# A macaron block (feed-forward, attention, feed-forward): the projections as sums of 16-bit products, and the rope sum one block later

## The chip, the cores and the metric

One Trainium2 chip, one of its cores. The metric is the device time of one execution in microseconds (us), as the median of several. In what follows PE is TensorE (PEld its weight loads), DVE is VectorE, ACT is ScalarE, POOL is GpSimd and SP is the engine that issues the DMAs.

## The reference

4 batches of 1024 rows of width 512 go through three residual layers. The first and the last are a feed-forward layer with ternary weights. The middle one is attention with 32 query heads and 8 key and value heads of 16 columns:

```
x = x + 0.5 * ffn(layernorm(x), w_gate_up, w_proj)
x = x + attn(layernorm(x), Wq, bq, Wk, bk, Wv, bv, Wo, bo)
x = x + 0.5 * ffn(layernorm(x), w_gate_up, w_proj)

Q, K, V = x @ Wq.T + bq, x @ Wk.T + bk, x @ Wv.T + bv
Q, K = Q * cos + rot_half(Q) * sin, K * cos + rot_half(K) * sin
out = softmax(Q @ K.T / 4) @ V @ Wo.T + bo
```

All of it is in 32-bit floats. The change concerns the line that makes Q, K and V.

## The kernel before, in words

The kernel runs five stages, one behind the other: `first_layer`, `projections`, `attention`, `attention_output` and `ffn`. Between them every engine waits for all the others.

**Projections** work on 32 blocks of 128 rows (`NSUB`). The 512 columns of a row meet a weight of 512 x 768 (`w_qkv`: `FQ` = 512 columns for the queries, then 128 for the keys, together `FA` = 640, then 128 for the values, in all `FALL` = 768). For one block these happen, with the line in brackets:

1. DVE takes the statistics of the rows (`row_stats`, L1312, and `row_moments`, L1316 and L1318), POOL the inverse root (`root`, L1363), DVE scales the rows (`normalise`, L1323).
2. PE turns the rows, four squares of 128 (`turn`, L1402), into PSUM (`turn_ps`), and ACT copies them to `xt` (`copy_turned`, L1384).
3. PE multiplies `xt` by `w_qkv` (`product`, L1411): for 512 and for 256 columns four matmuls each, on 32-bit operands. Each of these stands in the trace as two.
4. DVE adds the bias, 768 columns from PSUM (`add_bias`, L1331). SP stores the 128 columns of the values (L1287).
5. The rope: DVE multiplies 640 columns by the cosines (`cosine`, L1336), while POOL makes the sine terms in two operations of 320 columns (`sine`, L1372). DVE adds the two (`rotate`, L1343).
6. PE turns the 640 sums, five squares (`features`, L1420), ACT keeps a 16-bit part of them (`high_part`, L1391), DVE the 16-bit rest (`low_part`, L1348), and SP stores both for every second block (L1304). In the last eight steps SP also issues the first loads of the attention stage.

The order is written out by hand by `steps`: in step j each engine handles, for each stage of its list, the block j minus the stage's lag, in the order of the list. The first 8 steps and those behind the last block are written out, the 24 between are a loop of 8. DVE's list is

```
steps(nc, dve, NSUB, [(0, row_stats), (0, stats_made), (5, low_part), (0, row_moments),
                  (1, normalise), (3, add_bias), (3, cosine), (3, rotate)], unroll=RX, peel=RX)
```

PE has turn at 2, product at 3 and features at 4; ACT copy_turned at 2 and high_part at 5; POOL root at 0 and sine at 3. Semaphores count the blocks: `biased` is raised by add_bias and waited for by cosine and sine, `cosines` and `sines` by rotate, `roped` by features, `lows` (of the block before) by features.

**Balance.** In `first_layer`, while its second tile of 512 rows is worked on, the class `Balance` finds a power of two for the query weights and its inverse for the key weights: DVE takes largest magnitudes (`measure_queries`, `measure_rest`, L111 to L117), PE adds them over the partitions (`total_over_rows`, L122), DVE makes exponents and factors in a chain of operations on one or two columns (`take_factors`, L126 to L142) and later scales the weights (`apply`, L147). These stand between DVE's `hidden` operations (L413), one for each of the 16 parts of a tile.

Of the kernel before, what the change touches and what calls it, by code (L numbers as in the profile page):

```python
# [82 lines left out]
class Balance:  # L83
# [3 lines left out]
    def __init__(self, nc, ctx, w_qkv, bias, w_in, ones):  # L87
# [6 lines left out]
        self.parts = [(w_qkv[:, :, 0:FQ], bias[:, 0:FQ]), (w_qkv[:, :, FQ:FA], bias[:, FQ:FA])]  # L94
        self.w_in, self.ones = w_in, ones
        self.largest = sb("largest", [P, 4], F32)
        self.total = sb("total", [P, 4], F32)
        self.size = sb("size", [P, 2], F32)
        self.exponent = sb("exponent", [P, 2], mybir.dt.int32)
# [13 lines left out]
    def measure_rest(self, dve):  # L113
        w, b = self.parts[1]
        dve.tensor_reduce(self.largest[:, 1:2], w, AX.XY, ALU.max, apply_absolute_value=True).then_inc(self.measured, 1)
        for k in range(2):
            dve.tensor_reduce(self.largest[:, 2 + k:3 + k], self.parts[k][1], AX.X, ALU.max,  # L117
                              apply_absolute_value=True).then_inc(self.measured, 1)

    def total_over_rows(self, pe, ps):  # L120
        pe.wait_ge(self.measured, 4)
        pe.matmul(ps[:, 0:4], self.ones, self.largest[:], start=True, stop=True).then_inc(self.summed, 1)  # L122

    def take_factors(self, dve, ps):
        dve.wait_ge(self.summed, 1)
        dve.tensor_copy(self.total[:], ps[:, 0:4]).then_inc(self.copied, 1)  # L126
        dve.wait_ge(self.copied, 1)
        dve.tensor_tensor(self.size[:], self.total[:, 0:2], self.total[:, 2:4], ALU.add).then_inc(self.sizing, 1)
# [98 lines left out]
def first_layer(nc, units, squares, square, neg_half, wt, rows, src, dst, stored, ident, ones, hidden_range, balance,  # L227
# [12 lines left out]
    with ExitStack() as ctx:  # L240
# [130 lines left out]
        def _(dve):  # L371
# [90 lines left out]
            def tile(t, k, next_rows=True, c0=0):  # L462
                second = isinstance(t, int) and t == 1
                for c in range(c0, HC):
# [754 lines left out]
def projections(nc, x, rope, x_in, load, w_qkv, bias, w_in, qk_parts, v_rows, ident, neg_half,  # L1219
# [7 lines left out]
    with ExitStack() as ctx:  # L1227
# [81 lines left out]
        def _(dve):  # L1309
# [45 lines left out]
            steps(nc, dve, NSUB, [(0, row_stats), (0, stats_made), (5, low_part), (0, row_moments),  # L1355
                              (1, normalise), (3, add_bias), (3, cosine), (3, rotate)], unroll=RX, peel=RX)
# [608 lines left out]
def macaron(nc, x, units, w_qkv_t, b_qkv, w_o_t, b_o, rope, squares, out):  # L1965
# [8 lines left out]
    with ExitStack() as ctx:  # L1974
# [36 lines left out]
        with ExitStack() as outer:  # L2011
            output_in = OutputInput(nc, outer, ctx, rows, x1, att, den, inv)
            with ExitStack() as inner:
# [57 lines left out]
```

## Time and profile before

| | |
|---|---|
| median of 3 runs | 3099.67 us (3096.92 to 3100.73) |
| the profiled execution's own time | 3102.39 us |
| its span, first to last instruction | 3100.6 us, mean granted TensorE clock 0.982 of full |
| busy: PE, PEld, DVE, ACT, POOL | 2960.6, 1213.7, 1890.7, 1731.7, 749.6 us |
| `first_layer` | to about 779 us |
| `projections` | 779.7 to 1003 us |
| `attention` | to about 2265 us |
| `attention_output`, then `ffn` | to about 2385 us, then to the end |

The profile is of one execution, which took 2.72 us more than the median. Times in its rows are from the span's start. A row of the timeline reads: start, length of the run of like instructions, engine, line, operation, output and inputs, count, and in brackets how long the engine was idle before and what ended that. PE's lengths include the way through the array, so that successive ones overlap; the distance between starts is what one costs.

### The profile page before, as it was taken

Reading aid. Unit: us, or ns where it says so; the run is one execution under the profiler, and the core shown is the slowest. Engines: PE = TensorE matmul, PEld = TensorE weight load, DVE = VectorE, ACT = ScalarE, POOL = GpSimd, SP = SyncE. Lnnn points to the kernel's source line nnn. Section 1 sums busy time; section 2 is a strip of 40 time slices with the busy share of each in tenths; the row PEclk is TensorE's granted clock in tenths of the full one; section 3 lists DMA queues with packets and bytes.
Section 4 is the critical chain, followed back from the end, with each engine's and each line's share of the span. In section 5 each row is a group of like instructions: output and inputs, shape, how many; then the busy total and the mean of one; then the engine's idle time right before and its main releaser. Section 6 shows DMA issues by size and latency. Waiting matters only on the chain. (4 is left out here: it accounts for less than half of the span.)

```text
span 3100.6 us, 61131 instructions
## 1 busy us (share of the span) xinstructions
PE 2960.6 (95%) x20310; PEld 1213.7 (39%) x20310; DVE 1890.7 (61%) x2349; ACT 1731.7 (56%) x3156; POOL 749.6 (24%) x644
## 2 busy tenths in 40 slices
PE   7889999999998999999999999999997999999999
PEld 4444444444564122222222222222233444444444
DVE  7853222221676999999999999999723222222221
ACT  5733333333111599999999999999910333333332
POOL 0154444444443000000000000000022444444444
PEclk9999999999999799999999999999998999999999
DMA  4311110011333011111111111111256011111100
GB/s 132 116 43 41 41 41 14 26 41 42 92 106 102 11 34 31 30 30 30 31 31 30 30 30 30 30 31 31 95 181 227 5 42 41 41 41 41 41 14 28
DMA packets 163902, 160.56 MB, mean 52 GB/s; under 512 B 62552, under 2 KB 100824, under 8 KB 163808
## 3 DMA queue, kind: packets, MB, share of 16 engines
q1 hardware_dynamic: 163808, 159.30, 17.4%
q8 instruction: 60, 0.98, 0.1%
q14 instruction: 34, 0.28, 0.0%
HBM read 111.48 MB, written 47.19 MB: 51 GB/s over the span
## 5 line engine op out<-in xcount | busy, mean ns | idle before, releaser
L1756 DVE TENSOR_REDUCE at_neg_max<-at_max_ps 128x1 f32<-128x1024 f32 x1024 | 1172.6, 1206 | 19.8 <-PE at_max_ps L1634 19.0
L1742 ACT ACTIVATE at_probs<-at_score_ps 128x512 f32<-128x512 f32 x2048 | 1112.9, 597 | 81.9 <-PE at_score_ps L1654 37.8
L1663 PE MATMUL at_out_ps<-at_probs,at_v 128*32 128x256 f32 x8192 | 655.0, 391 | 24.4 <-ACT at_out L1728 24.0
L1634 PE MATMUL at_max_ps<-at_km,at_q 48*128 48x512 f16 x2048 | 633.0, 390 | 13.9 <-PEq L1227 8.2
L1654 PE MATMUL at_score_ps<-at_q,at_ks 50*128 50x512 f16 x2048 | 622.0, 382 | 15.0 <-DMA at_q<-at_max_parts 9.3
L983 DVE SCALAR_TENSOR_TENSOR f_h<-f_up_ps,hr_factor,f_gate 128x512 f32<-128x512 f32 x128 | 96.1, 751 | 478.1 <-ACT f_gate L1057 475.9
L1945 POOL TENSOR_TENSOR rows<-rows,bias 128x512 f32<-128x512 f32 x32 | 39.5, 1265 | 1353.2 <-ACTq L1880 1272.8
L1654 PEld LDWEIGHTS at_score_ps<-at_q,at_ks 50*128 50x128 f16 x2048 | 164.4, 93 | 434.8 <-ACT at_probs L1742 394.7
L413 DVE SCALAR_TENSOR_TENSOR f_h<-f_up_ps,hr_factor,f_gate 128x512 f32<-128x512 f32 x112 | 83.9, 749 | 393.9 <-PE f_up_ps L752 240.8
L1663 PEld LDWEIGHTS at_out_ps<-at_probs,at_v 128*32 128x32 f32 x8192 | 161.6, 108 | 402.1 <-issue 219.7
L1057 ACT ACTIVATE f_gate<-f_gate_ps 128x512 f32<-128x512 f32 x128 | 76.4, 597 | 354.3 <-PE f_up_ps L1130 354.3
L1079 POOL TENSOR_TENSOR f_h_lo<-f_h,f_h_hi 128x512 f16<-128x512 f32 x128 | 148.2, 1158 | 379.3 <-ACT f_h_hi L1046 379.3
L752 PE MATMUL f_gate_ps<-f_xt_hi,wt 128*128 128x512 f16 x512 | 195.7, 382 | 13.1 <-ACT f_gate L588 12.5
L770 PE MATMUL f_out_ps<-wt,f_h_hi 128*128 128x512 bf16 x512 | 195.0, 381 | 9.6 <-DVE rows L430 5.3
L661 POOL TENSOR_TENSOR f_h_lo<-f_h,f_h_hi 128x512 f16<-128x512 f32 x112 | 130.8, 1168 | 302.1 <-ACT f_h_hi L605 302.0
L1130 PE MATMUL f_gate_ps<-f_xt_hi,wt 128*128 128x512 f16 x512 | 195.1, 381 | 8.3 <-ACT f_gate L1057 6.9
L1144 PE MATMUL f_out_ps<-wt,f_h_hi 128*128 128x512 bf16 x512 | 194.1, 379 | 1.6 <-POOL f_h_lo L1079 1.6
L752 PE MATMUL f_gate_ps<-f_xt_lo,wt 128*128 128x512 f16 x512 | 195.3, 381 | 0.0
L770 PE MATMUL f_out_ps<-wt,f_h_lo 128*128 128x512 bf16 x512 | 195.1, 381 | 0.0
L1130 PE MATMUL f_gate_ps<-f_xt_lo,wt 128*128 128x512 f16 x512 | 195.1, 381 | 0.0
L1130 PE MATMUL f_up_ps<-f_xt_hi,wt 128*128 128x512 f16 x512 | 194.3, 379 | 0.0
L1130 PE MATMUL f_up_ps<-f_xt_lo,wt 128*128 128x512 f16 x512 | 194.1, 379 | 0.0
(148 smaller groups left out, 3722.5 us busy)
## 6 DMA issues: line engine op xcount, KB each, us to landing
rows<-x SPq DMA_DIRECT2D x40, 1024.0 KB, 5.6
x<-rows SPq DMA_DIRECT2D x16, 1024.0 KB, 4.6
f_raw<-units SPq DMA_DIRECT2D x48, 256.0 KB, 2.6
at_q<-qk_parts SPq DMA_DIRECT2D x384, 32.0 KB, 1.7
rows<-x SPq DMA_DIRECT2D x32, 256.0 KB, 2.8
at_q<-at_max_parts SPq DMA_DIRECT2D x512, 1.0 KB
att<-at_out SPq DMA_DIRECT2D x256, 32.0 KB
out<-rows SPq DMA_DIRECT2D x8, 1024.0 KB, 4.2
```

Source lines behind the costliest of these rows:

```text
L661: nc.gpsimd.tensor_tensor(h_lo[:, c % HR, :], h[:, c % HB, :], h_hi[:, c % HR, :], ALU.subtract).then_inc(hlos, 1)
L752: last = nc.tensor.matmul(ps[:], wt[:, 2 * c + n, d, :], part[:, k, d, :], start=(d == 0 and part is xt_hi), stop=(d == DC - 1 and part is ...
L770: last = nc.tensor.matmul(out_ps[s][:], part[:, c % HR, s * P:(s + 1) * P], wt[:, 2 * HC + (c // DC) * DC:2 * HC + (c // DC) * DC + DC, c ...
L983: nc.vector.scalar_tensor_tensor(out=h[:, c % HB, :], in0=up_ps[:], scalar=hidden_range.factor, in1=gate[:, c % 2, :], op0=ALU.mult, op1=A ...
L1079: nc.gpsimd.tensor_tensor(h_lo[:, c % HR, :], h[:, c % HB, :], h_hi[:, c % HR, :], ALU.subtract).then_inc(hlos, 1)
L1130: last = nc.tensor.matmul(ps[:], wt[:, 2 * c + n, d, :], part[:, k, d, :], start=(d == 0 and part is xt_hi), stop=(d == DC - 1 and part is ...
L1144: last = nc.tensor.matmul(out_ps[s][:], part[:, c % HR, s * P:(s + 1) * P], wt[:, 2 * HC + (c // DC) * DC:2 * HC + (c // DC) * DC + DC, c ...
L1634: done = nc.tensor.matmul(max_ps[u % 2][:, half * QB:(half + 1) * QB], q[k][rows, j // SLOTS, h * QB + c * P:h * QB + (c + 1) * P], km[k][ ...
L1654: nc.tensor.matmul(score_ps[pos % RING][:], ks[k][rows, kc * P:(kc + 1) * P], q[k][rows, j // SLOTS, h * QB:(h + 1) * QB], start=True, sto ...
L1663: last = nc.tensor.matmul(out_ps[2 * HD * j:2 * HD * (j + 1), cols], v[k][:, kc, :], probs[:, kc % PBUF, j, cols], start=(kc == 0 and part ...
L1742: nc.scalar.activation(probs[:, kc % PBUF, j, :], score_ps[pos % RING][:], ACT.Exp, scale=HD ** -0.5).then_inc(exps, 1)
L1756: nc.vector.tensor_reduce(neg_max[:, h, column:column + 1], max_ps[u % 2][:], AX.X, ALU.max, negate=True).then_inc(maxed, 1)
```

## The change

The operands of the product become 16-bit floats, each number as a high part and the rest. Of the four products of parts the one of the two rests is left out, so each matmul becomes three.

- The weights are split once, when the stage begins: ACT writes `w_hi` (two activations, 4 x 640 and 4 x 128 columns), DVE `w_lo` (`low_weights`, two operations), in its list behind `low_turned` of block 0. The weights are first multiplied by powers of two, one for queries and keys and one for the values, so that they fill the range of 16 bits. PE waits for both before its first product.
- Of each block ACT's copy now makes `xt_hi`, and a new DVE operation, `low_turned`, makes `xt_lo` from PSUM and `xt_hi`.
- `product` has 24 matmuls on 16-bit operands instead of 8 on 32-bit ones.
- `add_bias` also takes the power of two out again: two operations (640 and 128 columns) with a factor for each partition, instead of one of 768.
- DVE's list begins with low_turned at lag 2 and rotate at lag 4, where rotate stood last at lag 3.
- Balance measures the value weights and bias too (two more maxima) and makes the powers of two in a chain of seven small operations (`take_ranges`, in part 9 of the second tile).

```diff
+    def take_ranges(self, dve):
+        dve.tensor_tensor(self.top[:, 0:1], self.exponent[:, 1:2], self.exponent[:, 0:1],
+                          ALU.subtract).then_inc(self.sizing, 1)
+        dve.tensor_scalar(self.top[:, 1:2], self.exponent[:, 2:3], 0.0, None, ALU.add).then_inc(self.sizing, 1)
+        dve.wait_ge(self.sizing, 9)
+        dve.tensor_scalar(self.held[:], self.top[:], 20.0, 250.0, ALU.max, ALU.min).then_inc(self.sizing, 1)
...
+        dve.tensor_scalar(self.lowering_bits[:], self.lower_by[:], 23, None, ALU.logical_shift_left).then_inc(self.sizing, 1)
...
+                        if c == 9:
+                            balance.take_ranges(dve)
...
-                nc.vector.tensor_tensor(rows[:, k, :], row_ps[k][:, 0:FALL], bias, ALU.add).then_inc(biased, 1)
+                for n, (c0, c1) in enumerate(((0, FA), (FA, FALL))):
+                    last = nc.vector.scalar_tensor_tensor(
+                        out=rows[:, k, c0:c1], in0=row_ps[k][:, c0:c1], scalar=balance.lowering[:, n:n + 1],
+                        in1=bias[:, c0:c1], op0=ALU.mult, op1=ALU.add)
+                last.then_inc(biased, 1)
+
+            def low_weights(n, c0, c1):
+                dve.wait_ge(w_high, n + 1)
+                nc.vector.scalar_tensor_tensor(
+                    out=w_lo[:, :, c0:c1], in0=w_qkv[:, :, c0:c1], scalar=balance.raising[:, n:n + 1],
+                    in1=w_hi[:, :, c0:c1], op0=ALU.mult, op1=ALU.subtract).then_inc(w_low, 1)
+
+            def low_turned(i, k):
+                k %= 2
+                dve.wait_ge(turned_high, i + 1)
+                nc.vector.tensor_tensor(xt_lo[:, k], turn_ps[k][:], xt_hi[:, k], ALU.subtract).then_inc(copied, 1)
+                if isinstance(i, int) and i == 0:
+                    low_weights(0, 0, FA)
+                    low_weights(1, FA, FALL)
...
-            steps(nc, dve, NSUB, [(0, row_stats), (0, stats_made), (5, low_part), (0, row_moments),
-                              (1, normalise), (3, add_bias), (3, cosine), (3, rotate)], unroll=RX, peel=RX)
+            steps(nc, dve, NSUB, [(2, low_turned), (4, rotate), (0, row_stats), (0, stats_made), (5, low_part), (0, row_moments),
+                              (1, normalise), (3, add_bias), (3, cosine)], unroll=RX, peel=RX)
...
-                nc.scalar.copy(xt[:, k % 2], turn_ps[k % 2][:]).then_inc(copied, 1)
+                nc.scalar.copy(xt_hi[:, k % 2], turn_ps[k % 2][:]).then_inc(turned_high, 1)
...
+            for n, (c0, c1) in enumerate(((0, FA), (FA, FALL))):
+                nc.scalar.activation(w_hi[:, :, c0:c1], w_qkv[:, :, c0:c1], ACT.Copy,
+                                     scale=balance.raising[:, n:n + 1]).then_inc(w_high, 1)
...
+                if isinstance(i, int) and i == 0:
+                    pe.wait_ge(w_low, 2)
                 for c0, c1 in ((0, FQ), (FQ, FALL)):
                     for c in range(DC):
-                        last = nc.tensor.matmul(row_ps[k][:, c0:c1], xt[:, k, c, :], w_qkv[:, c, c0:c1],
-                                                start=(c == 0), stop=(c == DC - 1))
+                        for x_part, w_part in ((xt_hi, w_hi), (xt_hi, w_lo), (xt_lo, w_hi)):
+                            last = nc.tensor.matmul(row_ps[k][:, c0:c1], x_part[:, k, c, :], w_part[:, c, c0:c1],
```

How DVE's instructions stand in a step of the loop, before (from the bias sum of one block to the scaling of rows before the next bias sum; names are those of the code, and what a row waits for is in its brackets):

```order
L1331 TENSOR_TENSOR pj_rows<-pj_row_ps,bias 128x768 [waits pj_prods,pj_v_out0]
L1336 TENSOR_TENSOR pj_cosd<-pj_rows,pj_rope 128x640 [waits pj_biased]
L1343 TENSOR_TENSOR pj_cosd<-pj_cosd,pj_sind 128x640 [waits pj_sines,pj_cosines]
L1312 BN_STATS pj_stats<-rows 128x6 [waits pj_x_in4]
L1352 REGISTER_ALU
L1348 TENSOR_TENSOR pj_low<-pj_feat_ps,pj_high 128x5x128 [waits pj_highs,pj_stat]
L1316 BN_AGGR pj_mv<-pj_stats 128x2
L1318 TENSOR_SCALAR pj_var_eps<-pj_mv 128x1 [waits pj_aggr]
L1323 TENSOR_SCALAR rows<-rows,pj_mv,pj_rstd 128x512 [waits pj_rstds]
```

And the same stretch of DVE in the changed kernel:

```order
L1365 SCALAR_TENSOR_TENSOR pj_rows<-pj_row_ps,bl_lowering,bias 128x640 [waits pj_prods,pj_v_out1,pj_feats]
L1365 SCALAR_TENSOR_TENSOR pj_rows<-pj_row_ps,bl_lowering,bias 128x128
L1387 TENSOR_TENSOR pj_cosd<-pj_rows,pj_rope 128x640 [waits pj_biased]
L1379 TENSOR_TENSOR pj_xt_lo<-pj_turn_ps,pj_xt_hi 128x512 [waits pj_turned_high]
L1394 TENSOR_TENSOR pj_cosd<-pj_cosd,pj_sind 128x640 [waits pj_sines,pj_cosines]
L1345 BN_STATS pj_stats<-rows 128x6 [waits pj_x_in5]
L1403 REGISTER_ALU
L1399 TENSOR_TENSOR pj_low<-pj_feat_ps,pj_high 128x5x128 [waits pj_highs,pj_stat]
L1349 BN_AGGR pj_mv<-pj_stats 128x2
L1351 TENSOR_SCALAR pj_var_eps<-pj_mv 128x1 [waits pj_aggr]
L1356 TENSOR_SCALAR rows<-rows,pj_mv,pj_rstd 128x512 [waits pj_rstds]
```

The bias sum became two operations, and between the cosine product and the rope sum (L1343, now L1394) one operation more stands, low_turned (L1379). Otherwise the rope sum has the neighbours that it had.

DVE at the start of the stage in the changed kernel, from the scaling of block 0's rows to that of block 1's:

```order
L1356 TENSOR_SCALAR rows<-rows,pj_mv,pj_rstd 128x512 [waits pj_rstds]
L1379 TENSOR_TENSOR pj_xt_lo<-pj_turn_ps,pj_xt_hi 128x512 [waits pj_turned_high]
L1372 SCALAR_TENSOR_TENSOR pj_w_lo<-w_qkv,bl_raising,pj_w_hi 128x4x640 [waits pj_w_high]
L1372 SCALAR_TENSOR_TENSOR pj_w_lo<-w_qkv,bl_raising,pj_w_hi 128x4x128 [waits pj_w_high]
L1345 BN_STATS pj_stats<-rows 128x6 [waits pj_x_in2]
L1349 BN_AGGR pj_mv<-pj_stats 128x2 [waits pj_stat]
L1351 TENSOR_SCALAR pj_var_eps<-pj_mv 128x1 [waits pj_aggr]
L1356 TENSOR_SCALAR rows<-rows,pj_mv,pj_rstd 128x512 [waits pj_rstds]
```

Before, the second, third and fourth of these rows weren't there. PE turns block 1 before its first product, and waits for this last scaling.

## Rows read from the trace of the kernel before

**Rows 1.** Waits in the projection stage: who waits for whom, us, times, longest

```profile
DVE pj_cosd L1343 <- POOL pj_sind L1372: 52.7, 32, 1.9
...
DVE pj_rows L1331 <- PE pj_row_ps L1411: 9.9, 4, 7.4
```

**Rows 2.** Timeline of DVE and of POOL, one step of the loop

```profile
849.73 0.95 DVE L1331 TENSOR_TENSOR pj_rows<-pj_row_ps,bias 128x768 f32<-128x768 f32 x1
850.71 0.83 DVE L1336 TENSOR_TENSOR pj_cosd<-pj_rows,pj_rope 128x640 f32<-128x640 f32 x1
853.17 0.82 DVE L1343 TENSOR_TENSOR pj_cosd<-pj_cosd,pj_sind 128x640 f32<-128x640 f32 x1 [1.63 <-POOL pj_sind L1372]
...
856.10 0.95 DVE L1331 TENSOR_TENSOR pj_rows<-pj_row_ps,bias 128x768 f32<-128x768 f32 x1
...
850.76 2.31 POOL L1372 TENSOR_TENSOR pj_sind<-pj_rows,pj_rope 128x320 f32<-128x320 f32 x2 [0.55 <-DVE pj_rows L1331]
```

**Rows 3.** Timeline of PE: a step of the loop, then the first two full steps

```profile
849.23 0.74 PE L1420 MATMUL pj_feat_ps<-square,pj_cosd 128*128 128x128 f32 x5
849.87 0.66 PE L1402 MATMUL pj_turn_ps<-square,rows 128*128 128x128 f32 x4
850.36 5.33 PE L1411 MATMUL pj_row_ps<-w_qkv,pj_xt 128*128 128x512 f32 x16
...
792.89 5.33 PE L1411 MATMUL pj_row_ps<-w_qkv,pj_xt 128*128 128x512 f32 x16
...
799.04 5.33 PE L1411 MATMUL pj_row_ps<-w_qkv,pj_xt 128*128 128x512 f32 x16
```

**Rows 4.** Chain that ended last: eight 16-bit matmuls of 512 columns

```profile
2429.39 1.73 PE f_out_ps L1144 x8
```

**Rows 5.** Groups of DVE's instructions by form; behind the bar busy us, mean ns

```profile
L983 DVE SCALAR_TENSOR_TENSOR f_h<-f_up_ps,hr_factor,f_gate 128x512 f32<-128x512 f32 x128 | 96.1, 751 | 478.1 <-ACT f_gate L1057 475.9 <-issue 2.1
L974 DVE TENSOR_TENSOR f_xt_lo<-f_turn_ps,f_xt_hi 128x512 f16<-128x512 f32 x32 | 21.8, 682 | 3.1 <-ACT f_xt_hi L1040 3.1
L1764 DVE SCALAR_TENSOR_TENSOR at_max_parts<-at_score_ps,at_max_parts 16x128 f16<-16x128 f32 x64 | 17.8, 278 | 2.2
```

**Rows 6.** Timeline of DVE and POOL in the last layer, at the same time

```profile
2583.99 2.73 DVE L1000 SCALAR_TENSOR_TENSOR rows<-f_out_ps,f_inv,rows 128x512 f32<-128x512 f32 x4 [0.29 <-PE f_out_ps L1144]
...
2584.51 1.16 POOL L1079 TENSOR_TENSOR f_h_lo<-f_h,f_h_hi 128x512 f16<-128x512 f32 x1 [4.34 <-ACT f_h_hi L1046]
```

**Rows 7.** Timeline, start of the stage: DVE, ACT, PE

```profile
782.20 0.69 DVE L1312 BATCH_NORM_STATS2 pj_stats<-rows 128x6 f32<-128x512 f32 x1
...
783.09 0.58 ACT L1384 COPY pj_xt<-pj_turn_ps 128x512 f32<-128x512 f32 x1 [13.74 <-PE pj_turn_ps L1402]
783.80 1.11 PE L1402 MATMUL pj_turn_ps<-square,rows 128*128 128x128 f32 x4 [0.74 <-DVE rows L1323]
...
784.71 7.91 PE L1411 MATMUL pj_row_ps<-w_qkv,pj_xt 128*128 128x512 f32 x16
```

**Rows 8.** Timeline of DVE: first and last bias sum of the 32

```profile
792.66 0.96 DVE L1331 TENSOR_TENSOR pj_rows<-pj_row_ps,bias 128x768 f32<-128x768 f32 x1 [7.45 <-PE pj_row_ps L1411]
...
989.45 0.96 DVE L1331 TENSOR_TENSOR pj_rows<-pj_row_ps,bias 128x768 f32<-128x768 f32 x1 [0.70 <-PE pj_row_ps L1411]
```

**Rows 9.** Timeline of the DMA queue at the stage's end

```profile
990.43 0.37 SPq L1287 DMA_DIRECT2D v_rows<-pj_rows  x1
...
1002.71 0.53 SPq L1304 DMA_DIRECT2D qk_parts<-pj_low  x1
```

**Rows 10.** Timeline of DVE in part 10 of the second tile, first layer

```profile
228.92 0.75 DVE L413 SCALAR_TENSOR_TENSOR f_h<-f_up_ps,hr_factor,f_gate 128x512 f32<-128x512 f32 x1 [3.52 <-issue]
```

**Rows 11.** Windows: length, PE, PEld, DVE, ACT, POOL busy; granted clock, DMA share, GB/s

```profile
10.00:20.00 10.00, 7.57 (x39) 4.91 (x39) 8.59 (x23) 6.04 (x12) 1.31 (x1) 1.00 0.34 99
20.00:30.00 10.00, 6.46 (x39) 4.24 (x40) 7.44 (x18) 5.19 (x10) 0.00 (x0) 0.83 0.33 94
...
788.00:790.00 2.00, 2.00 (x4) 0.84 (x3) 0.00 (x0) 0.00 (x0) 0.00 (x0) 0.52 0.00 0
```

More of the change, by code:

```diff
@@ L92, in sem @@
             return ctx.enter_context(nc.semaphore(f"bl_{n}"))
-        self.parts = [(w_qkv[:, :, 0:FQ], bias[:, 0:FQ]), (w_qkv[:, :, FQ:FA], bias[:, FQ:FA])]
+        self.parts = [(w_qkv[:, :, c0:c1], bias[:, c0:c1]) for c0, c1 in ((0, FQ), (FQ, FA), (FA, FALL))]
         self.w_in, self.ones = w_in, ones
[L96 to L99, printed above, removed]
+        self.largest = sb("largest", [P, 6], F32)
+        self.total = sb("total", [P, 6], F32)
+        self.size = sb("size", [P, 3], F32)
+        self.exponent = sb("exponent", [P, 3], mybir.dt.int32)
+        self.top = sb("top", [P, 2], mybir.dt.int32)
+        self.held = sb("held", [P, 2], mybir.dt.int32)
+        self.raise_by = sb("raise_by", [P, 2], mybir.dt.int32)
+        self.lower_by = sb("lower_by", [P, 2], mybir.dt.int32)
+        self.raising_bits = sb("raising", [P, 2], mybir.dt.int32)
+        self.lowering_bits = sb("lowering", [P, 2], mybir.dt.int32)
+        self.raising, self.lowering = self.raising_bits[:].bitcast(F32), self.lowering_bits[:].bitcast(F32)
         self.half = sb("half", [P, 1], mybir.dt.int32)
@@ L113, in measure_rest @@
     def measure_rest(self, dve):
[L114 to L117, printed above, removed]
+        for k in (1, 2):
+            dve.tensor_reduce(self.largest[:, k:k + 1], self.parts[k][0], AX.XY, ALU.max,
+                              apply_absolute_value=True).then_inc(self.measured, 1)
+        for k in range(3):
+            dve.tensor_reduce(self.largest[:, 3 + k:4 + k], self.parts[k][1], AX.X, ALU.max,
                               apply_absolute_value=True).then_inc(self.measured, 1)
     def total_over_rows(self, pe, ps):
-        pe.wait_ge(self.measured, 4)
-        pe.matmul(ps[:, 0:4], self.ones, self.largest[:], start=True, stop=True).then_inc(self.summed, 1)
+        pe.wait_ge(self.measured, 6)
+        pe.matmul(ps[:, 0:6], self.ones, self.largest[:], start=True, stop=True).then_inc(self.summed, 1)
     def take_factors(self, dve, ps):
         dve.wait_ge(self.summed, 1)
-        dve.tensor_copy(self.total[:], ps[:, 0:4]).then_inc(self.copied, 1)
+        dve.tensor_copy(self.total[:], ps[:, 0:6]).then_inc(self.copied, 1)
         dve.wait_ge(self.copied, 1)
-        dve.tensor_tensor(self.size[:], self.total[:, 0:2], self.total[:, 2:4], ALU.add).then_inc(self.sizing, 1)
+        dve.tensor_tensor(self.size[:], self.total[:, 0:3], self.total[:, 3:6], ALU.add).then_inc(self.sizing, 1)
         dve.wait_ge(self.sizing, 1)
@@ L1216, in projection_loads, with projections @@
     return rope, x_in, load
-def projections(nc, x, rope, x_in, load, w_qkv, bias, w_in, qk_parts, v_rows, ident, neg_half,
+def projections(nc, x, rope, x_in, load, w_qkv, balance, bias, w_in, qk_parts, v_rows, ident, neg_half,
                 before, n_starts, start_next, v_out, parts_out):
@@ L1246, in projections @@
         low = sb("low", [P, 2, NF, 2 * P], F16)
+        w_hi = sb("w_hi", [P, DC, FALL], F16)
+        w_lo = sb("w_lo", [P, DC, FALL], F16)
         turn_ps = [bank(f"turn_ps{k}", [P, DC, P]) for k in range(2)]
@@ L2017, in macaron @@
                 attention_in = AttentionInput(nc, inner, qk_parts, v_rows)
-                projections(nc, rows, pj_rope, pj_in, pj_load, w_qkv, bias[:, 0:FALL], w_in, qk_parts, v_rows,
+                projections(nc, rows, pj_rope, pj_in, pj_load, w_qkv, balance, bias[:, 0:FALL], w_in, qk_parts, v_rows,
                             ident, neg_half, [(f_stored[0], NTILE * 16)], attention_in.STARTS, attention_in.start,
```

14 lines of the change are left out of this document (13 added, 1 removed).

## The prediction
> **What bounds the kernel now.** The stages don't overlap, and outside `projections` the change adds only a few small operations in `first_layer`; so the question is what sets the pace of a block in the projections. PE looks like the bound there: its product alone takes 5.33 us of a step of 6.37 [rows 3]. I checked that against the waits, then against one step of the timeline.
>
> The waits say otherwise: DVE's rope sum waits for POOL's sine terms in every one of the 32 blocks, 52.7 us in all, while DVE's bias sum waits for PE only four times [rows 1]. The timeline shows a closed ring [rows 2]. The bias sum starts at 849.73 and the cosine product at 850.71 (0.98 later). POOL starts then too, takes 2.31, and the rope sum starts at 853.17 (2.46 behind the cosine product, 1.63 of it idle). Then DVE goes through rope sum, statistics, low_part, moments and normalise without a gap, and the next bias sum starts at 856.10 (2.93). 0.98 + 2.46 + 2.93 = 6.37 us a block, with no wait for PE in it. PE needs less: in the first full steps products follow each other at 6.15 (792.89 to 799.04), and in the loop its step reads 0.64 for the features, 0.49 for the turn and the rest for the product [rows 3]. PE is close behind, but the ring DVE, POOL, DVE is the bound.
>
> **The product.** Eight matmuls on 32 bits go, 24 on 16 bits come. In the last layer eight of 512 columns take 1.73 us, 0.216 each [rows 4]. The stage has none of 256; I take half, 0.108 (bounds 0.108 and 0.216). Product: 12 x 0.216 + 12 x 0.108 = 3.89, at most 5.18. PE's step becomes 0.64 + 0.49 + 3.89 = 5.02 (at most 6.31), where it had 6.15. The 1.13 us gained lie beside the ring: worth nothing in the loop, since PE wasn't waited for. Only where DVE did wait for PE is there a gain: the three short waits of the bias sum, 9.9 - 7.4 = 2.5 us [rows 1], in the last steps, where DVE has no statistics left to take. **-2.5 us.** (With the upper bound this gain goes and nothing else changes.)
>
> **The rope sum one block later.** The list gives it lag 4 instead of 3, but it also moves from the end of a step to the beginning of the next. The order of DVE's instructions shows what that comes to: bias sum, cosine product, low_turned, rope sum. It still comes before the next block's bias sum, which is what the next sine terms wait for. So the ring stays closed, and low_turned is all that slips into the 1.63 us of waiting.
>
> **low_turned.** Like the 682 ns one of the last layer [rows 5], 0.59 from start to start. Reached 0.74 behind the cosine product's start, it ends by 1.42, against 2.46 at which the rope sum may start: 1 us of cover is left. It needs ACT's copy of the turned rows: PE's turn starts 0.14 behind the bias sum and takes 0.66 [rows 2, 3], the copy 0.58 [rows 7], so it is done near 1.4, and DVE comes to low_turned at 1.17 + 0.74 = 1.9. **0 us**; without that cover, 0.59 x 30.
>
> **The bias sum in two.** An operation of this kind, with a factor for each partition and a PSUM source, takes 751 ns for 512 columns [rows 5]; the plain one takes 0.95 for 768 [rows 2] and 0.682 for 512, so a column is 1.05 ns, and the fixed part is 0.15 plain and 0.22 here. Then 640 columns take 0.88 and 128 take 0.35. Four such in a row take 2.73 [rows 6], so the next starts 0.09 before the end. Until the cosine product: 0.88 - 0.09 + 0.35 + 0.03 = 1.17, where it was 0.98. That is +0.19 in each of 31 intervals, **+5.9 us**. Bounds: the 128-column row of 278 ns gives 0.12 (+3.7); no overlap of the two, and 0.05 more, gives 0.35 (+10.9). I take the middle, since the 751 ns row is the same operation with the same kind of factor. This term stands in the ring, in front of both the cosine product and POOL, so nothing hides it.
>
> The Trainium skill, "VectorE: DVE Perf Modes", section on the TRN2 errata, gives a PSUM-source operation 120 cycles plus one a column, whatever the operation; by that the pair would cost only about 0.04 us more than the single one, +1 us in all, and the sum below would be near +3. The rows of this kernel show the fixed part to differ by 0.07 between the two kinds, and I go by them.
>
> **The start.** ACT splits the weights in the idle time before its first copy (13.74 us idle before 783.09 [rows 7], though the stage begins only at 779.7): two activations, an estimated 3.2 us by the size of its other ones. That just fits. DVE's share doesn't. Behind low_turned of block 0 (783.75 to 784.35) it makes w_lo: 2560 columns at 1.05 ns and 0.2 fixed, 2.87, and 512 columns, 0.75. Less the overlaps that lasts until 787.8, and only then come the statistics of block 2 and the scaling of block 1, which were at 782.20 before and let PE turn block 1 at 783.80, 1.6 later [rows 7]. That turn stands ahead of the first product. So it starts at 789.35 instead of 783.80, 5.55 later, and the product at 790.3. That product runs with the granted clock at about half, as the first did before (0.52 until 790 [rows 11]). Before: 7.91 us instead of 5.33; with C us at half speed, C + (10.24 - C) / 2 = 7.7, C = 5.2. Now 24 matmuls are 7.78 at half speed; after 5.2 of them 1.3 remain at full: 6.5, done at 796.8. The first bias sum was at 792.66 [rows 8]: **+4.1 us** (2.8 if the clock rises after 2.5 us, 5.4 if only behind the product).
>
> **The end.** Behind the last values' store at 990.43 SP issues without a gap until 1002.71 [rows 9]; that store waits for the last bias sum. So the end of the stage moves as the last bias sum does, one to one. Those 12.8 us hold 24 issues, 0.53 each; between two of the last bias sums SP has at most nine, 4.8 us, and steps then take 5.2: no new wait.
>
> **first_layer.** Two more maxima cover 640 columns, under the 0.95 of the 768-column row. The seven small operations cost at most 0.28 each by the small row of [rows 5], 2.0 together, and one of them may be held up by a POOL operation of 1.16 [rows 6]; DVE was idle 3.52 there [rows 10]. **0 us**. Were the cover gone, PE would wait for the next hidden part by the overrun, once, at most 1 us or so.
>
> **Sum.** 4.1 + 5.9 - 2.5 = **+7.5 us**. Against the profiled execution's own time: 3102.4 + 7.5 = 3109.9. It lies 2.7 above the median of the runs, so for the median 3099.7 + 7.5 = 3107.2. I say 3107. Bounds: 2.8 + 3.7 - 2.5 = +4 to 5.4 + 10.9 - 2.5 = +14, and +1 with the page's cost. A measurement of this kernel can tell about 0.2%, 6.2 us, from no change, and that lies inside.
>
> **Rivals.**
> - *A, the later rope sum does hide the sine terms* (faster). Then nothing in the step waits for POOL, and DVE's own work is the bound: 6.37 - 1.63 + 0.59 + 0.19 = 5.52 a block, 0.85 less in 30 or 31 blocks, -26, and +4.1 at the start: 3078. It decides on whether the sine terms are ready 1.4 us behind the start of the cosine product; now they take 2.46 [rows 2]. For it: this is what a lag of a block would give had another block's bias sum stood between. Against: the order of instructions. The same figure would result were PE the bound in truth. 12%.
> - *B, low_turned and POOL's sine terms get in each other's way* (slower). POOL's two sine operations take 2.31 together. Were the second held up for low_turned's 0.59, the ring would be longer by that in 30 blocks: +18, 3125. Against: four DVE operations with one PSUM and one SBUF input run while POOL takes 1.16 for its operation [rows 6], as long as always. 8%.
> - *C, PE's clock falls* (slower). PE will be busy 5.02 of 6.56 us, 77%, idle in one piece before the features. In the first layer 7.57 of 10 busy had the full clock, 6.46 of 10 a mean of 0.83 [rows 11]. At half speed a block would take PE 10 us. But then PE is busy without a pause, as at the start, where 5.2 us so brought the clock back; such a spell costs PE 2.6 and its slack of 1.5 a block takes most of it: about +1 a spell, a spell in every other block +16, 3123. The Trainium skill, "TensorE: Matmul & The Clock Gate", section "A second HAM failure mode: psum-queue depth-cycling", speaks for this rival: short pauses between groups of matmuls make the clock go back and forth. Whether it holds for pauses of this size no row here settles. 8%.
> - The forecast holds in the remaining 72%, of which 28 within 6.2 us and 44 above.
>
> **How the numbers follow.** Faster 0.12 (A). Same 0.28. Slower 0.44 + 0.16 = 0.60. The range 3100 to 3119 takes in the forecast's bounds up to the runs' scatter and the weak forms of B and C; left out are A and full B and C.
>
> **What would show it.** Right: the rope sum still waits for POOL in every block, about 1.0 us instead of 1.63; bias sums 6.56 apart; no wait of the bias sum for PE behind the first block; PE idle about 1.4 us before the features; first product at 790.3; in all PE's busy share of the stage falls and the time doesn't. Wrong: bias sums 5.5 apart and no wait for POOL (A); POOL's pair at 2.9 instead of 2.31 (B); a granted clock under 1.00 in the loop (C); the two bias operations adding 0.05 instead of 0.19.

## The result, and the profile after

| | before | after |
|---|---|---|
| median of the runs, us | 3101.18 (3096.74 to 3104.39, 20 runs) | 3107.3 (3105.16 to 3111.02, 20 runs) |
| ratio after / before | | 1.0022, 95% interval 1.0016 to 1.0028 |
| the profiled execution's own time, us | 3102.4 | 3106.08 |

The change makes the kernel slower by 0.22%, 6.1 us by the medians (5.0 to 8.7 us by the interval of the ratio). PE is busy for 36.5 us less than before (2960.6 us), and the time hasn't followed. From the page of the profile, busy us of each engine and share of the span:

```profile
PE 2924.1 (94%) x20566; PEld 1193.0 (38%) x20566; DVE 1922.6 (62%) x2424; ACT 1734.7 (56%) x3158; POOL 752.1 (24%) x644
```

The waits in the stage (us in all, times, longest) answer to [rows 1]:

```profile
PE pj_feat_ps L1478 <- DVE pj_low L1399: 42.9, 31, 4.4
DVE pj_cosd L1394 <- POOL pj_sind L1423: 34.2, 32, 1.6
DVE pj_rows L1365 <- PE pj_row_ps L1468: 2.6, 1, 2.6
```

DVE's rope sum still waits for POOL's sine terms 32 times; DVE waits for a product once, the first. PE now stands idle in front of the features of nearly every block (31 times). The timeline of one step of the loop (start, duration, what it does, idle time before and its releaser) answers to [rows 2, 3]:

```profile
848.08 1.14 DVE L1365 SCALAR_TENSOR_TENSOR pj_rows<-pj_row_ps,bl_lowering,bias 128x640 f32<-128x640 f32 x2
848.71 0.38 PE L1468 MATMUL pj_row_ps<-pj_w_hi,pj_xt_hi 128*128 128x512 f16 x1
849.25 0.82 DVE L1387 TENSOR_TENSOR pj_cosd<-pj_rows,pj_rope 128x640 f32<-128x640 f32 x1
849.29 2.30 POOL L1423 TENSOR_TENSOR pj_sind<-pj_rows,pj_rope 128x320 f32<-128x320 f32 x2 [0.73 <-DVE pj_rows L1365]
849.99 0.68 DVE L1379 TENSOR_TENSOR pj_xt_lo<-pj_turn_ps,pj_xt_hi 128x512 f16<-128x512 f32 x1
851.70 0.83 DVE L1394 TENSOR_TENSOR pj_cosd<-pj_cosd,pj_sind 128x640 f32<-128x640 f32 x1 [1.03 <-POOL pj_sind L1423]
...
852.50 0.27 PE L1468 MATMUL pj_row_ps<-pj_w_hi,pj_xt_lo 128*128 128x256 f16 x1
...
854.14 0.74 PE L1478 MATMUL pj_feat_ps<-square,pj_cosd 128*128 128x128 f32 x5 [1.37 <-DVE pj_low L1399]
854.64 1.14 DVE L1365 SCALAR_TENSOR_TENSOR pj_rows<-pj_row_ps,bl_lowering,bias 128x640 f32<-128x640 f32 x2
```

The ring is still there: bias sum to cosine product 1.17, cosine product to rope sum 2.45 (1.03 of it idle), rope sum to the next bias sum 2.94; together 6.56 us, where it was 6.37. low_turned sits inside the wait for POOL. PE is done with its product 3.90 us after it began and has nothing to do for 1.4.

The first steps of the stage, the same timeline, answer to [rows 7]:

```profile
780.06 0.69 DVE L1345 BATCH_NORM_STATS2 pj_stats<-rows 128x6 f32<-128x512 f32 x1 [0.96 <-PEq L265]
...
784.65 3.54 DVE L1372 SCALAR_TENSOR_TENSOR pj_w_lo<-w_qkv,bl_raising,pj_w_hi 128x2560 f16<-128x2560 f32 x2
...
789.71 1.12 PE L1456 MATMUL pj_turn_ps<-square,rows 128*128 128x128 f32 x4 [6.32 <-DVE rows L1356]
790.62 0.63 PE L1468 MATMUL pj_row_ps<-pj_w_hi,pj_xt_hi 128*128 128x512 f16 x1
796.21 1.15 DVE L1365 SCALAR_TENSOR_TENSOR pj_rows<-pj_row_ps,bl_lowering,bias 128x640 f32<-128x640 f32 x2 [2.58 <-PE pj_row_ps L1468]
```

PE waits 6.32 us for the scaling of block 1, which stands on DVE behind the splitting of the weights. Against [rows 8] the first bias sum starts 3.55 later (3.2, if the 0.33 by which the whole stage begins later in this execution is taken off). The last bias sum and attention's first matmul, and behind them that matmul in the kernel before:

```profile
995.30 1.14 DVE L1365 SCALAR_TENSOR_TENSOR pj_rows<-pj_row_ps,bl_lowering,bias 128x640 f32<-128x640 f32 x2
...
1010.23 1.04 PE L1692 MATMUL at_max_ps<-at_km,at_q 48*128 48x512 f16 x4 [8.31 <-PEq L1254]
```

```profile
1003.98 1.04 PE L1634 MATMUL at_max_ps<-at_km,at_q 48*128 48x512 f16 x4 [8.18 <-PEq L1227]
```

The last bias sum starts 5.85 later than in [rows 8]. Attention's first matmul comes 6.25 later, so with the 0.33 taken off the stage is 5.9 longer. The two profiled spans differ by less, 3.7 us, because the stages behind took 2.5 less in that one execution; the medians of 20 runs differ by 6.1, about as the stage does.

### The profile page after: what moved, and what is told of

It is laid out like the page before. It is cut to its first block and busy times, and to the rows that moved or that the text cites. A ratio compares the mean times of both kernels' runs of the same rounds, so it can differ in the third digit from the quotient of the medians.

```text
span 3104.3 us, 61727 instructions
## 1 busy us (share of the span) xinstructions
PE 2924.1 (94%) x20566; PEld 1193.0 (38%) x20566; DVE 1922.6 (62%) x2424; ACT 1734.7 (56%) x3158; POOL 752.1 (24%) x644
## 3 DMA queue, kind: packets, MB, share of 16 engines
q1 hardware_dynamic: 163808, 159.30, 17.5%
```

## The experiments

Two questions. First, is the bound the ring (bias sum, sine terms, rope sum, next bias sum), as the prediction says, or is it PE or DVE's own work (rival A, and the guess that one reads off the busy shares)? Second, what does each part of the change cost by itself? Each kernel was timed beside the kernel before on the same chip; a ratio is to that one, with its 95% interval. The kernel before had medians of 3099.90, 3100.49 and 3100.99 us beside these runs and 3101.18 in the result, so a difference between medians that were not taken side by side is uncertain by 1 us or more; where it matters, the traces of the stage are given too. In the lists of DVE's steps a number is the lag in blocks.

**Opening the ring in the changed kernel.** The rope sum goes behind low_part of the same step, three entries further down the list (two pieces of work, the statistics and low_part; `stats_made` is only a wait). The list's lag stays 4, nothing else changes:

```diff
-[(2, low_turned), (4, rotate), (0, row_stats), (0, stats_made), (5, low_part), (0, row_moments),
+[(2, low_turned), (0, row_stats), (0, stats_made), (5, low_part), (4, rotate), (0, row_moments),
                   (1, normalise), (3, add_bias), (3, cosine)]
```

> The changed kernel with the rope sum moved further down DVE's list, behind low_part (lag 4 as in the change). Ring theory: the sine terms (2.46 us from the cosine product's start) are ready when DVE gets to the rope sum (about 2.8 us behind it), so the wait of 1.03 us goes, bias sums stand 5.45 apart instead of 6.56, and the time is some 33 us shorter than the changed kernel's, near 3074. PE theory (PE sets the pace whatever DVE does): no change, 3107. Between them: if low_part or the features come too late because of the new place, the period is between 5.5 and 6.5 and PE or ACT is named as what DVE waits for.

Measured: 3072.45 us (3070.0 to 3075.01), ratio 0.9912 (0.9897 to 0.9927). DVE in a step of this kernel's timeline:

```profile
851.18 1.14 DVE L1365 SCALAR_TENSOR_TENSOR pj_rows<-pj_row_ps,bl_lowering,bias 128x640 f32<-128x640 f32 x2
852.35 0.82 DVE L1387 TENSOR_TENSOR pj_cosd<-pj_rows,pj_rope 128x640 f32<-128x640 f32 x1
...
855.15 0.82 DVE L1394 TENSOR_TENSOR pj_cosd<-pj_cosd,pj_sind 128x640 f32<-128x640 f32 x1
856.62 1.14 DVE L1365 SCALAR_TENSOR_TENSOR pj_rows<-pj_row_ps,bl_lowering,bias 128x640 f32<-128x640 f32 x2
```

The rope sum starts 2.80 behind the cosine product, when the sine terms are there, and waits for nothing; bias sums come 5.44 apart instead of 6.56. The work is the same to the last operation. From the first bias sum to the last it takes 166.44 us instead of 199.09, 32.7 less: 27 of the 31 intervals are 1.12 shorter, the first one and the last three 2.3 together. The medians differ by 34.9, some 2 us more than the traces show, and where these lie is open. So what held the changed kernel was the place of one operation in DVE's order. What sets the pace now is DVE's own work: it has no gap in the step of 5.44, while PE's step was 5.03 in the changed kernel.

**Opening it in the kernel before.** There the rope sum goes from lag 3 at the end to the same place, lag 4 behind low_part, with the product still on 32 bits:

```diff
-[(0, row_stats), (0, stats_made), (5, low_part), (0, row_moments), (1, normalise),
- (3, add_bias), (3, cosine), (3, rotate)]
+[(0, row_stats), (0, stats_made), (5, low_part), (4, rotate), (0, row_moments), (1, normalise),
+ (3, add_bias), (3, cosine)]
```

> The kernel before (32-bit product) with the rope sum at lag 4 behind low_part. Ring theory: DVE then has about 5.1 us a block, PE 6.15, so PE becomes the bound with bias sums 6.15 apart instead of 6.37 and waits of the bias sum for PE in nearly every block; 28 x 0.22 = 6 us faster than before, near 3095. PE theory: PE was the bound already, no change. If the ring were all that held the stage, the gain would be 1.3 us a block, 35 us.

Measured: 3092.45 us (3089.12 to 3094.25), ratio 0.9976 (0.9967 to 0.9985). The waits of DVE in the stage, and two bias sums of the timeline:

```profile
DVE pj_rows L1331 <- PE pj_row_ps L1411: 41.7, 32, 5.8
DVE pj_cosd L1343 <- POOL pj_sind L1372: 8.1, 29, 1.1
```

```profile
852.18 0.96 DVE L1331 TENSOR_TENSOR pj_rows<-pj_row_ps,bias 128x768 f32<-128x768 f32 x1 [1.10 <-PE pj_row_ps L1411]
...
858.35 0.96 DVE L1331 TENSOR_TENSOR pj_rows<-pj_row_ps,bias 128x768 f32<-128x768 f32 x1 [1.15 <-PE pj_row_ps L1411]
```

With the ring open PE is the bound: every bias sum waits for a product, and the step is PE's, 6.17 here and 6.15 on average, which is what the prediction had read for it. Only 0.2 of the 6.37 could be had here. So, with the ring open, the whole change (the 16-bit product with all its extra work) gains 3092.5 - 3072.5 = 20 us, two kernels timed side by side; with the ring closed it costs 6.

**The changed kernel with the old place of the rope sum.** Lag 3, at the end of the step, so that low_turned is no longer between cosine product and rope sum:

```diff
-[(2, low_turned), (4, rotate), (0, row_stats), ..., (3, add_bias), (3, cosine)]
+[(2, low_turned), (0, row_stats), ..., (3, add_bias), (3, cosine), (3, rotate)]
```

> The changed kernel with the rope sum where it was before (lag 3, last in the list), low_turned first in the list. Ring theory: low_turned comes out from under the wait, the rope sum waits 1.63 us again, bias sums 6.56 + 0.59 = 7.15 apart, +18 us on the changed kernel, near 3125. Theory that the place of the rope sum is worth nothing: 3107.

Measured: 3124.83 us (3123.57 to 3126.5), ratio 1.0082 (1.0066 to 1.0097). From its timeline:

```profile
850.24 0.82 DVE L1394 TENSOR_TENSOR pj_cosd<-pj_cosd,pj_sind 128x640 f32<-128x640 f32 x1 [1.63 <-POOL pj_sind L1423]
...
853.77 1.14 DVE L1365 SCALAR_TENSOR_TENSOR pj_rows<-pj_row_ps,bl_lowering,bias 128x640 f32<-128x640 f32 x2
...
860.93 1.14 DVE L1365 SCALAR_TENSOR_TENSOR pj_rows<-pj_row_ps,bl_lowering,bias 128x640 f32<-128x640 f32 x2
```

The wait is 1.63 again, as before the change, and the step 7.16: low_turned lies bare in the ring and costs 0.60 in each. That is what the move of the rope sum buys: cover for low_turned, 17.5 us. It doesn't hide the sine terms.

**The move alone, in the kernel before.** `(3, rotate)` at the end becomes `(4, rotate)` at the front, and nothing else:

> The kernel before with only the change's move of the rope sum (lag 4, first in the list), 32-bit product. Ring theory: DVE's order of instructions is the same but for the first and last steps, bias sums 6.37 apart, the wait for the sine terms 1.63 us in each block, no change within 0.1%. Theory that a lag of one block hides the sine terms: wait gone, PE at 6.15, 6 us faster.

Measured: 3098.67 us (3095.14 to 3103.03), ratio 0.9996 (0.9986 to 1.0005). Bias sums at 847.90, 854.28 and 860.66, 6.38 apart as ever, and this wait:

```profile
DVE pj_cosd L1343 <- POOL pj_sind L1372: 52.2, 32, 1.6
```

A lag of one block more, and every instruction has the neighbours it had.

**The product alone.** The changed kernel with its product back on 32-bit operands; the splitting of the rows and weights is still done but not used, the factor of the bias sums is 1, and all places in the lists are kept:

```diff
-for x_part, w_part in ((xt_hi, w_hi), (xt_hi, w_lo), (xt_lo, w_hi)):
-    last = nc.tensor.matmul(row_ps[k][:, c0:c1], x_part[:, k, c, :], w_part[:, c, c0:c1],
...
+last = nc.tensor.matmul(row_ps[k][:, c0:c1], xt[:, k, c, :], w_qkv[:, c, c0:c1],
+                        start=(c == 0), stop=(c == DC - 1))
```

> The changed kernel with only the product back on 32-bit operands (8 matmuls, unscaled weights, the factor in the bias sum set to one); low_turned, w_hi, w_lo and the two bias sums stay. Ring theory: PE needs 6.15 us a step again, still under the ring's 6.56, so bias sums stay 6.56 apart in the loop; only the first product (7.7 instead of 5.5) and the last three steps (5.7 to 6.1 instead of 5.1 to 5.6) cost: some 4 to 5 us more than the changed kernel, near 3112. Theory that the 16-bit product is worth its own time in the loop: 1.25 x 32 = 40 us more, 3147.

Measured: 3109.73 us (3105.57 to 3113.05), ratio 1.0029 (1.0019 to 1.0038). Its last three bias sums in the timeline:

```profile
987.68 1.14 DVE L1365 SCALAR_TENSOR_TENSOR pj_rows<-pj_row_ps,square,bias 128x640 f32<-128x640 f32 x2 [0.45 <-PE pj_row_ps L1467]
...
993.83 1.14 DVE L1365 SCALAR_TENSOR_TENSOR pj_rows<-pj_row_ps,square,bias 128x640 f32<-128x640 f32 x2 [0.95 <-PE pj_row_ps L1467]
...
999.54 1.14 DVE L1365 SCALAR_TENSOR_TENSOR pj_rows<-pj_row_ps,square,bias 128x640 f32<-128x640 f32 x2 [0.52 <-PE pj_row_ps L1467]
```

In the loop the bias sums are 6.56 apart (869.83, 876.39), to the hundredth the step of the changed kernel, with a product that takes some 1.1 us longer. The three waits at the end, 1.9 us, are there again, and from the first bias sum to the last it takes 201.31 us instead of 199.09: 2.2 more, where the prediction's term is 2.5. The first product is slower too: the first bias sum stands 17.51 behind the beginning of the stage instead of 16.15, 1.4 more. Together that is 3.6 us for the stage. The medians differ by 2.4 and the intervals of their ratios overlap, so it is the unchanged step and these stretches that show what the faster product is worth with the ring closed, and not the medians.

**One bias sum instead of two.** One power of two for all 768 columns, the raising factor of the weights too, and one operation:

```diff
-for n, (c0, c1) in enumerate(((0, FA), (FA, FALL))):
-    last = nc.vector.scalar_tensor_tensor(
-        out=rows[:, k, c0:c1], in0=row_ps[k][:, c0:c1], scalar=balance.lowering[:, n:n + 1],
-        in1=bias[:, c0:c1], op0=ALU.mult, op1=ALU.add)
+nc.vector.scalar_tensor_tensor(
+    out=rows[:, k, :], in0=row_ps[k][:, 0:FALL], scalar=balance.lowering[:, 0:1],
+    in1=bias, op0=ALU.mult, op1=ALU.add)
```

> The changed kernel with one bias sum of 768 columns again, still with a factor for each partition, and one power of two for all weights. If the size of the term is right (0.22 fixed with a factor, 0.15 without, 1.05 ns a column), the one operation takes 1.02 us and 1.05 to the cosine product, so bias sums are 6.44 apart instead of 6.56: 3.7 us less than the changed kernel, near 3103.5. Rival, the cost is all in there being two operations: 6.37 apart, 6 us less. Rival, it is all in the factor: 6.56, no gain.

Measured: 3101.11 us (3095.74 to 3104.32), ratio 0.9998 (0.9989 to 1.0007). The group of this operation by form (busy us, mean ns), and two of them in the timeline:

```profile
L1364 DVE SCALAR_TENSOR_TENSOR pj_rows<-pj_row_ps,bl_lowering,bias 128x768 f32<-128x768 f32 x32 | 32.4, 1012 | 2.7 <-PE pj_row_ps L1466 2.7
```

```profile
868.08 1.01 DVE L1364 SCALAR_TENSOR_TENSOR pj_rows<-pj_row_ps,bl_lowering,bias 128x768 f32<-128x768 f32 x1
...
874.52 1.01 DVE L1364 SCALAR_TENSOR_TENSOR pj_rows<-pj_row_ps,bl_lowering,bias 128x768 f32<-128x768 f32 x1
```

The step is 6.44, 0.12 less, as expected, and from the first bias sum to the last it takes 195.19 us instead of 199.09: 3.9 less. Of the 0.19 that the pair adds to a step, 0.12 is thus for there being two operations and 0.07 for the factor. The median is 6.2 below that of the changed kernel, which is 2.3 more than the stage shows. The intervals of the ratios come as near as 1.0016 and 1.0007, a distance of 3 us, so 3.9 fits them; whether anything else is in the rest stays open.

**The start, two ways.** First, low_turned of block 0 and the splitting of w_lo behind the scaling of block 1, so that PE's turn of block 1 needn't wait for them:

```diff
     def normalise(i, k):
...
+        if isinstance(i, int) and i == 1:
+            low_turned(0, 0, True)
```

> The changed kernel with DVE's low_turned of block 0 and w_lo moved behind the scaling of block 1's rows. Start theory: PE's turn of block 1 goes back to about 784.1, and the first product waits for w_lo alone: it starts near 788.2 instead of 790.4, everything behind it 2.3 us earlier, near 3105. If the first product had been held by w_lo itself and not by the turn behind it, no change.

Measured: 3105.82 us (3103.39 to 3110.89), ratio 1.0018 (1.0009 to 1.0027). The first product in the timeline, and the windows around its end (length, PE, PEld, DVE, ACT, POOL busy, then granted clock, DMA share, GB/s):

```profile
787.66 0.59 PE L1472 MATMUL pj_row_ps<-pj_w_hi,pj_xt_hi 128*128 128x512 f16 x1 [3.09 <-DVE pj_w_lo L1374]
```

```profile
790.00:792.00 2.00, 2.00 (x6) 0.73 (x5) 0.00 (x0) 0.00 (x0) 0.00 (x0) 0.50 0.00 0
792.00:794.00 2.00, 2.00 (x14) 1.29 (x13) 0.00 (x0) 0.00 (x0) 0.00 (x0) 0.76 0.00 0
```

The product starts 8.28 us behind the beginning of the stage instead of 10.56, as expected. But the first bias sum starts only 1.2 earlier (14.99 instead of 16.15 behind it). The product ran at the half clock until about 792.7, 5.0 us, where the changed kernel's ran so for 3.0. So an earlier product isn't an earlier end of it in the same measure, and of the expected 2.3 us the trace shows half. The medians don't decide this: they differ by 1.5, with overlapping intervals (1.0009 to 1.0027, and 1.0016 to 1.0028).

Second, the split done already in the first layer, in five pieces on ACT and DVE in its third tile, in memory that six of the sixteen hidden parts give back:

```diff
+    if isinstance(t, int) and t == 2 and 4 <= c < 9:
+        balance.low_weights(dve, c - 4)
...
+    if isinstance(t, int) and t == 2 and 3 <= c < 8:
+        balance.high_weights(act, c - 3)
```

> The changed kernel with the weights split one tile earlier, in the first layer's third tile, in five pieces on ACT and on DVE in their idle time. Start theory: the projections' first product starts near 785.0 instead of 790.4 and, with 5.2 us at half clock, the first bias sum near 791.5 instead of 796.2: 4.7 us less than the changed kernel, near 3102.5, if the first layer is not made longer. If the pieces delay the first layer's activations, part of that comes back there: up to 1 us a piece.

Measured: 3102.07 us (3099.44 to 3106.7), ratio 1.0006 (0.9997 to 1.0015). PE's waits in the first layer are those of the changed kernel to 0.2 us each. The time is as expected and the way there was not. From its timeline:

```profile
781.82 0.69 DVE L1370 BATCH_NORM_STATS2 pj_stats<-rows 128x6 f32<-128x512 f32 x1 [0.96 <-PEq L286]
...
785.81 0.69 DVE L1398 TENSOR_TENSOR pj_xt_lo<-pj_turn_ps,pj_xt_hi 128x512 f16<-128x512 f32 x1 [1.43 <-ACT pj_xt_hi L1451]
...
788.02 1.12 PE L1469 MATMUL pj_turn_ps<-square,rows 128*128 128x128 f32 x4 [2.86 <-DVE rows L1381]
```

The product comes 7.1 us behind the beginning of the stage (788.93), not 5.2: DVE reaches low_turned of block 0 before ACT's copy is made, waits 1.43 for it, and the scaling of block 1 stands behind. I had overlooked that a wait stays where the split had been. The first bias sum, 12.83 behind the beginning instead of 16.15, is 3.3 earlier, where 4.7 was expected; that the medians differ by 5.2 nevertheless isn't explained by the stage.

**Both together.** The opened ring with the early split:

> Both together: the rope sum behind low_part (ring open) and the weights split in the first layer. Gains should add, since one is in the loop and one ahead of it: 3072.5 - 4.7 = 3068, 1.0% under the kernel before. If the clock at the start decides otherwise, between 3066 and 3072.

Measured: 3072.01 us (3068.24 to 3075.24), ratio 0.9902 (0.9887 to 0.9918). From the beginning of the stage to attention's first matmul it takes 194.6 us, 3.3 less than with the opened ring alone (197.9), but the medians of four runs each, 3072.01 and 3072.45, don't show it. The expected 3068 was missed, and with four runs that range over 7 us the time can't say whether the two gains add.

Then with one bias sum, one power of two, and low_turned of block 0 behind the scaling of block 1:

> best_early with one bias sum and one power of two for all weights, and low_turned of block 0 behind the scaling of block 1's rows. Bias sums 5.31 to 5.33 apart instead of 5.45 (DVE's work is the bound), -3.7; the first product starts 5.2 us behind the stage's beginning instead of 7.1, of which the half clock takes some back, -1 to -2. Near 3067 if best_early is at 3072; the parts ahead of and in the loop add. If PE (5.02 and its waits for DVE) has become the bound, the period stays at 5.45.

Measured: 3064.18 us (3063.51 to 3065.99), ratio 0.9882 (0.9866 to 0.9898): 1.2% below the kernel before, 1.4% below the changed one, and 2.8 us below the expectation. From its timeline:

```profile
786.92 1.06 PE L1481 MATMUL pj_row_ps<-bl_kept,pj_xt_hi 128*128 128x512 f16 x2
...
851.77 1.01 DVE L1391 SCALAR_TENSOR_TENSOR pj_rows<-pj_row_ps,bl_lowering,bias 128x768 f32<-128x768 f32 x1
857.09 1.01 DVE L1391 SCALAR_TENSOR_TENSOR pj_rows<-pj_row_ps,bl_lowering,bias 128x768 f32<-128x768 f32 x1
```

Bias sums are 5.32 apart: the 0.12 that one bias sum saves DVE comes off the step in full, as it must if DVE's own work is the bound. The product starts 5.0 us behind the beginning of the stage (781.94), the place that I had wrongly expected of the early split alone. From that beginning to attention's first matmul it takes 189.2 us, 5.5 less than with both together; the medians differ by 7.8, and the rest isn't located.

## Why the prediction was right

It forecast +7.5 us and so 3107, and the median is 3107.3. The change measured is +6.1 us (5.0 to 8.7). That the figure itself was met to 0.3 us is luck: the prediction added its 7.5 to a median of three runs, 3099.7, and the median of 20 is 3101.18; these 1.5 us made up for the 1.4 by which the forecast change was too large. The path that it named is not luck. Step by step:

- **The ring and the rope sum.** This was right. The rope sum waits 1.03 in each step ("about 1.0"), steps are 6.56 apart, and the lag alone changes nothing, in the kernel before either (6.38).
- **low_turned at nothing.** This was right, and its condition too: without that place it costs 0.60 a step.
- **The product.** It was forecast at 3.89 and takes 3.90: the matmuls stand 0.216 and 0.109 apart, half the columns in half the time. PE's step is 5.03 (features 847.58, next work for it done at 852.61). Its gain is hidden but for the waits at the end, 2.2 us from the first to the last bias sum where 2.5 was forecast, and the share of the first product, which is in the term of the start.
- **The bias sum in two.** A step of the loop is longer by the +0.19 that was forecast (6.56 for 6.37). Over the loop less came: the first 28 intervals take 183.3 us instead of 178.8, +4.5 where 28 times 0.19 are 5.3, because nine of them were 6.46 to 6.60 long in that execution of the kernel before; in the kernel before with the move alone they take 178.1, which gives +5.2. The durations of the two operations (min, median, max of both forms together):

```profile
L1365 DVE SCALAR_TENSOR_TENSOR pj_rows<-pj_row_ps,bl_lowering,bias x64: 339/610/883, 796.2 to 996.1; 128x640 f32<-128x640 f32 x32, 128x128 f32<-128x128 f32 x32
```

  They are 339 and 883 ns, forecast 350 and 880. The single one with a factor takes 1012 for 768 columns, and the plain sum 0.95 to 0.96 [rows 2, 8]: about 0.06 more by the kind of operation (forecast 0.07). The Trainium skill ("VectorE: DVE Perf Modes", the section on the TRN2 errata) gives both kinds one fixed part; an estimate from it is that the pair costs 0.04 more than the one, and the step is 6.41. The measurement decides: 6.56.
- **The start.** The forecast was +4.1, and the profiled executions differ by 3.2. The places were right (turn 789.71 for 789.35, product 790.62 for 790.3, with a stage that begins 0.33 later; ACT's two activations take 3.04 for 3.2). The term mis-sized is the time at half clock: 5.2 us taken from the kernel before, 3.0 measured. Windows (length, PE, PEld, DVE, ACT, POOL busy, then granted clock, DMA share, GB/s):

```profile
790.00:792.00 2.00, 2.00 (x8) 1.11 (x8) 0.52 (x1) 0.59 (x1) 0.05 (x1) 0.50 0.00 0
792.00:794.00 2.00, 2.00 (x7) 0.72 (x6) 1.56 (x5) 0.00 (x0) 0.74 (x1) 0.59 0.00 0
794.00:796.00 2.00, 2.00 (x16) 1.47 (x15) 0.00 (x0) 0.00 (x0) 0.03 (x1) 1.00 0.00 0
...
860.00:880.00 20.00, 15.66 (x99) 9.80 (x99) 16.51 (x31) 3.54 (x6) 9.25 (x9) 1.00 0.33 99
```

  The product took 5.4 instead of 6.5. But the other side of the difference moves as much. In the profiled execution of the kernel before the first bias sum stands 12.93 behind the beginning of the stage, and in the kernel before with the move alone, where nothing ahead of that point differs, 11.28 (stage from 779.86):

```profile
791.14 0.96 DVE L1331 TENSOR_TENSOR pj_rows<-pj_row_ps,bias 128x768 f32<-128x768 f32 x1 [5.80 <-PE pj_row_ps L1411]
```

  Against that one the start costs 4.9. So the term is 3.2 to 4.9 by the execution that one compares with, and that 4.1 lies between is no proof of its working.
- **The end.** It moves nearly one to one: last bias sum +5.85, attention +6.25. The last two steps are 5.1 long (985.09, 990.20, 995.30), the forecast 5.2.
- **first_layer at nothing.** This was right: DVE still waits 0.68 for PE in front of part 10, where it had been idle 3.52 [rows 10]. Two of the small operations took as long as a POOL operation beside them (1.14 each), not one as forecast. The whole chain used 2.8 of the cover, within the 2.0 + 1.16 that the prediction allowed.
- **The sum.** The whole stage, from its beginning to attention's first matmul, takes 230.2 us instead of 224.3 in the profiled execution of the kernel before and 221.9 in that of the move alone: +5.9 or +8.3, and the forecast 7.5 lies between.
- **The rivals.** *Rival A* fell: it needed the rope sum behind other work, and got low_turned alone. Its price was right for the kernel in which that does happen: steps of 5.52 named, 5.44 measured, 3078 named, 3072 measured. *Rival B* fell: POOL's pair takes 2.30 (2.31 before), with low_turned running beside it. *Rival C* fell: the last of the windows above has PE 78% busy, with a pause in every step, at a clock of 1.00. The Trainium skill ("TensorE: Matmul & The Clock Gate", section "A second HAM failure mode: psum-queue depth-cycling") tells of a kernel in which short pauses between groups of matmuls make the clock go back and forth; with pauses of 1.4 us every 6.56 nothing of that shows here.

## What to carry to other kernels

PE needed 6.15 of a step of 6.37 and wasn't the bound: look for the operation that waits in every step, and follow it round to itself. A lag in a software pipeline moves nothing by itself; what counts is which operations stand, in each engine's order, between a result's request and its use. Put the work that is independent there first, and only then make the product faster: the same change cost 6 us with the ring closed and gained 20 with it open. The product by itself was tried with the ring closed only, where it is worth 2.4 us by the medians and 3.6 by the stage.

## What the runs showed of the hardware

- The same first product of the kernel before, at the same place, took 7.91 us in one execution [rows 7] and 6.26 in another (the opened ring in that kernel, where nothing before that point differs):

```profile
784.90 6.26 PE L1411 MATMUL pj_row_ps<-w_qkv,pj_xt 128*128 128x512 f32 x16
```

  Its time at half clock isn't a constant to build on: worked out from these two lengths against 5.33 it was 5.2 and 1.9 us; in the changed kernels it was 3.0 (product from 790.62) and 5.0 (from 787.66). What decides it wasn't tried.
- low_turned (one PSUM, one SBUF input) ran beside POOL's sine terms and neither was longer for it (0.68 and 2.30 us). Two of the small operations of the new powers of two, of one or two columns, took 1.14 us where another took 0.14, and each ended with the POOL operation that ran beside it (226.75 and 227.97), which reads as DVE being held up by POOL; no run takes POOL's work away to prove it. The kernel before has two such in its own chain (0.92 us from 220.32 and 1.20 from 221.28, beside POOL operations that end at 221.23 and 222.46). From the changed kernel's timeline, first layer:

```profile
225.53 1.22 POOL L688 TENSOR_TENSOR f_h_lo<-f_h,f_h_hi 128x512 f16<-128x512 f32 x1 [2.77 <-ACT f_h_hi L632]
225.63 1.14 DVE L156 TENSOR_TENSOR bl_top<-bl_exponent 128x1 int32<-128x1 int32 x1
226.69 0.14 DVE L158 TENSOR_SCALAR bl_top<-bl_exponent 128x1 int32<-128x1 int32 x1
226.71 1.26 POOL L698 TENSOR_TENSOR f_sqsum<-f_sqsum,f_sq 128x512 f32<-128x512 f32 x1
226.87 1.14 DVE L160 TENSOR_SCALAR bl_held<-bl_top 128x2 int32<-128x2 int32 x1
```
